# Moving two runs of small attention products within a token tile's projections

## The reference

```python
x = x + _L0_attn_ref(_layernorm(x, axis=-1), ...)
x = x + _L0_ffn_ref(_layernorm(x, axis=-1), ...)
# attention, H = 32 heads of D = 32; per token s the scores are a 32 x 32 matrix
q = (hidden_states @ wq.T + bq).reshape(B, S, H, D)     # k and v likewise
scores = jnp.einsum('bshd,bstd->bsht', q, k) / np.sqrt(D).astype(np.float32)
probs = jax.nn.softmax(scores, axis=-1)
context = jnp.einsum('bsht,bstd->bshd', probs, v).reshape(B, S, E)
# feed forward, three weight matrices rounded to the NF4 code in blocks of 64
h = jax.nn.silu(gate) * up
```

## Time and profile before

| | us |
|---|---|
| median of 3 runs | 1895.08 |
| lowest, highest | 1891.53, 1898.92 |
| the profiled execution | 1894.59 |
| its span | 1892.7 |
| TensorE busy (matmul) | 1831.2 |
| VectorE busy | 1729.0 |
| ScalarE busy | 1378.0 |
| GpSimd busy | 1252.9 |

### The profile page before, as it was taken

One profiled execution on the slowest core, in us unless ns is written; L12 is line 12 of the kernel. 1 busy time (PEld: TensorE's weight loads), 2 busy tenths in 40 slices (PEclk: granted clock), 3 DMA queues, 4 the chain that ended last, 5 costly groups with the idle time before them and its releaser, 6 DMA issues. The chain is left out here.

```text
span 1892.7 us, 42748 instructions
## 1 busy us (share of the span) xinstructions
PE 1831.2 (97%) x16470; PEld 884.2 (47%) x16470; DVE 1729.0 (91%) x1848; ACT 1378.0 (73%) x1523; POOL 1252.9 (66%) x706
## 2 busy tenths in 40 slices
PE   6899999999989999999999999999999999999998
PEld 6555555555434344444444444444444444444443
DVE  6799999999888999999999999999999999999985
ACT  7233333333359898898998988989989889898881
POOL 0134534534647887977878779778787787787961
PEclk9999999999999999999999999999999999999999
DMA  9346666665587131221122212212211221131115
GB/s 322 123 128 188 169 173 198 170 174 157 133 215 239 41 66 45 45 62 49 44 52 47 56 44 50 61 44 50 61 44 44 50 61 44 44 65 42 39 29 190
DMA packets 252925, 182.76 MB, mean 97 GB/s; under 512 B 177792, under 2 KB 220800, under 8 KB 252800
## 3 DMA queue, kind: packets, MB, share of 16 engines
q1 hardware_dynamic: 221600, 167.28, 31.8%
q10 hardware_dynamic: 31200, 13.64, 3.5%
HBM read 114.29 MB, written 24.12 MB: 73 GB/s over the span
## 5 line engine op out<-in xcount | busy, mean ns | idle before, releaser
L1718 DVE SCALAR_TENSOR_TENSOR bank<-signs,bank 128x1024 f32<-128x1024 int8 (+2 forms) x756 | 919.9, 1217 | 53.2 <-ACT signs L1584 25.8
L1878 PE MATMUL bank<-x2T,w12T 128*128 128x512 f16 x4128 | 896.3, 380 | 8.3 <-DMA x2T<-x_lo_dram 5.9
L1878 PEld LDWEIGHTS bank<-x2T,w12T 128*128 128x128 f16 x4128 | 403.9, 98 | 497.5 <-DMA x2T<-x_lo_dram 6.4
L1584 ACT ACTIVATE signs<-w_first,compare_bias 128x1024 int8<-128x1024 f32 (+1 forms) x588 | 630.6, 1138 | 1.5 <-DVE bank L1718 1.1
L1584 ACT ACTIVATE signs<-w_last,compare_bias 128x1024 int8<-128x1024 f32 (+2 forms) x294 | 314.4, 1119 | 0.8 <-DVE w_first L1718 0.6
L1068 PE MATMUL bank<-wT,xT_hi 128*128 128x512 f16 x768 | 294.8, 384 | 2.4 <-PEq L321 2.4
L1068 PE MATMUL bank<-wT,xT_lo 128*128 128x512 f16 x768 | 294.1, 383 | 2.0 <-issue 2.0
L1906 PE MATMUL bank<-w3T_hi,hT_hi 128*128 128x512 f16 x672 | 255.3, 380 | 7.5 <-DMA w3T_lo<-half 4.7
L1907 PE MATMUL bank<-w3T_lo,hT_hi 128*128 128x512 f16 x672 | 255.4, 380 | 0.0
L1908 PE MATMUL bank<-w3T_hi,hT_lo 128*128 128x512 f16 x672 | 255.4, 380 | 0.0
L1498 POOL TENSOR_TENSOR acc<-acc,hidden 128x512 f32<-128x512 f32 x160 | 201.1, 1274 | 27.5 <-ACT hidden L1625 26.7
(11 more groups left out here) (140 smaller groups left out, 2142.7 us busy)
## 6 DMA issues: line engine op xcount, KB each, us to landing
ff_raw<-in_L_ffn_w SPq DMA_DIRECT2D x63, 512.0 KB, 4.6
w_first<-in_L_ffn_w SPq DMA_DIRECT2D x41, 512.0 KB, 3.8
w_last<-in_L_ffn_w SPq DMA_DIRECT2D x19, 512.0 KB, 4.0
x_nat<-in_L_attn_hidden_states SPq DMA_DIRECT2D x16, 512.0 KB, 5.8
x_res<-in_L_attn_hidden_states SPq DMA_DIRECT2D x16, 512.0 KB, 5.3
x<-x_res SPq DMA_DIRECT2D x16, 512.0 KB, 3.6
acc<-x SPq DMA_DIRECT2D x4, 2048.0 KB, 8.2
out<-acc SPq DMA_DIRECT2D x15, 512.0 KB, 2.6
```

The costliest lines, as they stand in the source:

```text
L1584: nc.scalar.activation(signs[0:rows, ring(v, k), 0:cols], w_nat(v % SLOTS)[0:rows, 0:cols], ACT.Sign, scale=COMPARE[SUMMED[k]][0], bias=co ...
L1718: V.scalar_tensor_tensor(to, part, HALF_STEP[SUMMED[k]], total, ALU.mult, ALU.add).then_inc(sign_used, 1)
L1878: last = nc.tensor.matmul(dst, w, tokens_of(sb_, x)[:, :, c], start=c == 0 and i == 0, stop=c == C - 1 and i == 2)
```

## The change

On TensorE alone, two calls move. The second half of the scores (`score_part(n, end, HALF, QUAD)`) stood between the two halves of Q; it now stands after Q, ahead of the turn. The second half of the context (`mix_part(n, HALF, QUAD)`) stood between K and V; it now stands between the two halves of V. In the last tile but one it follows the first `next(ahead)`.

```diff
-                def score_second():
-                    score_part(n, end, HALF, QUAD)
-
                 def mix_first():
                     mix_part(n, 0, HALF)
 
-                def ahead_half():
-                    next(ahead)
+                def mix_second():
+                    if ahead:
+                        next(ahead)
+                    if attend:
+                        mix_part(n, HALF, QUAD)
 
                 if project:
                     pe.wait_ge(x_lo_done, 2 * n + 2)
                     if attend:
                         score_part(n, end, 0, HALF)
-                    project_one(n, u, it, 0, with_lo, score_second if attend else None)
+                    project_one(n, u, it, 0, with_lo)
+                    if attend:
+                        score_part(n, end, HALF, QUAD)
                 if normalize:
                     pe.wait_ge(normed, n + 2)
                     turn(x_nat[:, 1 - u], x_turned)
                 if project:
                     project_one(n, u, it, 1, with_lo, mix_first if attend else None)
-                    if attend:
-                        mix_part(n, HALF, QUAD)
-                    project_one(n, u, it, 2, with_lo, ahead_half if ahead else None)
+                    project_one(n, u, it, 2, with_lo, mix_second)
```

## The result

The changed kernel takes **1898.88 us** (20 runs, 1896.28 to 1903.39), the kernel before 1895.06 (20 runs, 1891.53 to 1901.64). The ratio is 1.0021 with a 95% interval of 1.0014 to 1.0027: 4 us slower, and within the 0.5% that were called "the same". The forecast was 1900.0 with a range of 1889 to 1911. The profiled execution is the fastest of its runs, 1896.28 us with a span of 1894.5, so it shows 1.8 us more span than before and not the 3.8 us of the medians. The windows tell where the difference lies.

What follows compares the result with a forecast made beforehand. TensorE, busy 97% of the span, was taken to bound the kernel, with idle time at the turn and at late instruction blocks. Terms -2.1 + 3.0 + 5.8 - 1.5 gave +5.2 us, so 1900 us, range 1889 to 1911.

Steps and rivals of the forecast that it cites:

- What bounds it: Whole kernel: TensorE, busy 97% of the span; only idle at the tile turn and stops 128 pairs apart can change.
- The cuts that go (-2.1): Stops in the second context half (252.15, 420.24) and second score half (as 323.09) vanish: -2.1 us.
- the floor: Turn of the next tile: TensorE waits for VectorE's normalization, so up to about 0.65 us lost after V1 is free.
- New borders elsewhere (+3.0): New stops in or behind second context halves (first step, 284, 453) and second scores (354): +3.0 us, bounds 0.8 and 5.
- my rule: Instruction fetch: a block's arrival is counted from entering the block before, 2.8 to 4.3 us quiet, 5.8 to 6.2 full.
- The seam (+5.8): Between steps, 4.8 us cover instead of 8.2 cuts the first scores by 1.0 us in ten steps: +5.8 us (0 to 16).
- The low clock (-1.5): After the stop at 459.72 the granted clock fell to 0.51; this was counted to go: -1.5 us.
- The sum: Whole kernel: -2.1 + 3.0 + 5.8 - 1.5 = +5.2 us, giving 1900 us against the median 1895.08.
- Quick blocks: Rival at the seam: blocks arrive at the quiet price, both first-score stops go; -2.6 us, 1892.5 us, chance 0.22.
- Waiting until the full stretch ends: Rival at the seam: blocks wait for the DMA-full stretch's end, stops 1.9 us on average; +16, 1911 us, chance 0.18.
- Hidden fetches: Rival, whole kernel: all instruction fetches are hidden, cuts have another origin, order is neutral; 1895 us, chance 0.05.
- VectorE late: Rival: the second context's 0.9 us margin before weighing is used up, V1's evacuation slips 0.5 us in 12 steps; 1906 us, chance 0.04.

Runs made afterwards that it cites:

- S2 alone: Kernel before with only the second half of the scores moved behind Q, the second half of the context left between K and V: 1894.93 us, ratio 0.9995.
- with 8 matmuls: Changed kernel with the second context half behind the 8th matmul of V's second half, 8 matmuls before the next step's first scores: 1910.31 us, ratio 1.0093.

## Why the prediction was right, point by point

- **What bounds it.** Right. The parts of a step cost the same wherever they stand, stops of 128 pairs' distance and the turn's wait are what moves (with 1.3 us of low clock), there are 58 packets on q8 in the twelve steps, and the feed forward did not change (1435.27 and 1435.26 us).
- **The cuts that go (-2.1).** Right in place: M2 is whole at 250 and 420 us and S2's cut at 323.09 is gone. The contexts' stops in the twelve steps went from 2.9 us to nothing; with S2's 0.6 that is -3.5 before the floor takes its part. It is more than the 2.1 I had because the two stops in M1 (0.8 us each, at 218.66 and 388.73) went too. Their borders did not move and the 16 matmuls ahead of M1 stayed, so by my reading they should have stood, and with S2 alone they do (0.36 us at 217.70, 0.72 at 388.89); why they went here is open. One stop is new that I had not seen, 1.86 us at 321.25: it is the block after the one that S1 waited for at pair 5 (316.97), 128 pairs on.
- **New borders elsewhere (+3.0).** This step failed: none of the four stops came. M2 of the first step, S2 at 355.20 and what follows 283 and 453 run through (282.04 and 453.96 above are whole, with no stop behind them). I had given all borders in quiet stretches the price of those that stopped. The instruction queue shows more. q8 in 279.5 to 281.2, the second row in 287.3 to 288.6; from 281.2 to 287 it has no packet:

```profile
q8 instruction: 1, 0.02, 3.4%
...
q8 instruction: 1, 0.02, 5.3%
```

  The packet of 287.3 brings the block that S1 waits for at pair 111. So the one of 279.9 brings the block entered behind M2, at 283.2. By my rule it is asked for when the block before it is entered, 282.0; it moved two microseconds earlier. Here 32 long matmuls lie ahead of M2, and the request runs ahead of TensorE's own work. That reading rests on the order of the packets; no kernel here tested it by itself.
- **The seam (+5.8).** The place and the sign were right, and so was the size of 5.8 to 6.2 us for a block: 5.8 on average, 5.2 to 6.6 in single steps. That it is a price of the block wasn't: the packets start when the full stretch ends, and M2's place in it makes that 5.8. Ten steps of the twelve have a stop there, as I had put it, of 10.9 us in all, and 1.3 of it stood there before: +9.6. The floor gave back 4.6 (the turn's waits) where I had 4.2. That leaves +5.0, against the forecast's 5.8.
- **The low clock (-1.5).** It is gone behind 461.16, but a stretch like it stands behind another stop, 1.65 us at 201.91: 1.3 us in the twelve steps. And behind them it comes back by other stops: the 31 us from 458.73 on have a mean granted clock of 0.95, as the same 31 us had before, with M2 of the last tile but one standing late behind a transpose that waits 2.4 us (L1924) where it waited 0.6. The term was taken for a property of one place. It isn't one, nor does it follow from a stop's length alone: behind the longer stops of 1.86 us at 289.81 and 321.25 the granted clock stayed at 1.00, as the second row has it for the first of them. What decides between them no run here shows.

```profile
458.73:490.00 31.27, 27.66 (x613) 14.77 (x612) 29.62 (x43) 12.12 (x13) 13.25 (x8) 0.95 0.52 153
...
290.00:293.00 3.00, 3.00 (x30) 1.41 (x19) 2.80 (x7) 0.00 (x0) 0.57 (x2) 1.00 0.64 197
```

- **The sum.** +5.2 was forecast. In the twelve steps it is +5.0 (seam) - 3.5 (cuts that went) + 0.9 (projections) + 1.3 (low clock) = +3.7, and 3.64 in the windows. Two terms failed, +3.0 that came to nothing and -1.5 that came to +1.3, with opposite signs, and a third, -2.1, gave 1.4 more than forecast; a good part of the match to 0.1% is that, and so luck.
- **The rivals.** Quick blocks: no, S1 is cut in eleven steps. Waiting until the full stretch ends: this is the mechanism that the packets show. Its time was too high because it put the end 0.2 us behind S1's start; in the changed kernel's eleven cut steps the stretch ends from 1.6 us before to 0.5 us behind it, 0.5 before on average, and the stops are 1.1 and not 1.9 us. So the forecast had the right time with a fixed price that isn't one. Hidden fetches: no. A time near 1895 under S2 alone is what the Trainium skill's rule would give (page "Runtime: NRT & Kernel Launch", section "Instruction fetch mechanics": mostly hidden); there stops of 4.0 us in the scores still stand, so the agreement in time is not one in mechanism. VectorE late: not in the change, where the turn's waits fell; with 8 matmuls it is.

## What to carry to other kernels

On this kernel a dense run of tiny matmuls uses a fetched block of 128 load and matmul pairs in 1.3 us, while its successor came 2.8 to 6.6 us after the block was entered. Count what lies between such a run and the next, in microseconds of long instructions, and look at what the DMA does meanwhile: here a block asked for in a full stretch came at its end, and it is that end, and not a fixed time, which the next run has to stand behind; an even spacing is worth nothing if the short gap falls in the busy stretch. Before believing a gain of a few tenths of a per cent from moved instructions, shift all of them by half a block and measure again; and see what the next engine's floor leaves of it.

## What the runs showed that was not expected

- A shift of half a block (64 pairs, 0.6 us of work) made the kernel before 0.34% slower, some 6 us, and the changed kernel by 0.1%, within its noise.
- A block can come early: the packet for a border at 283.2 us moved at 279.9, ahead of the border before it. With a run just behind, it comes after the entry.
- A block's packet starts when the full stretch of other transfers ends, within 0.6 us in 21 of 22 cuts, whether the block was entered 0.9 or 4.1 us before; TensorE goes on 1.2 to 1.6 us after the packet's end. Entered later in the stretch, a block took 4.8 instead of 5.8 us on average.
- A change between the large and the small matmuls costs about 0.2 us a piece, so mixing them finely is dearer than the stops that it avoids.
- Spells at the lower clock followed single stops: 1.65 us at 201.91 in the changed kernel, and 1.82 us at 289.06 with S2 alone (0.50 from 289.70 to 292.70). They did not follow each long one, as 1.86 us at 289.81 in the changed kernel shows.
